# q projected two tiles ahead, in front of V, with a semaphore of its own for V's projections

## The chip, the cores and the metric

The kernel runs on one core of a Trainium2 chip. The metric is the device time of one execution in microseconds (us). A core has five engines that run beside each other and meet at semaphores: TensorE (PE; its weight loads are PEld), VectorE (DVE), ScalarE (ACT), GpSimd (POOL) and SyncE (SP, which here issues DMAs). Each takes its own instructions strictly in the order in which the program gives them.

## The reference

Four residual blocks run over x [1, 2048, 128]: an attention, a feed-forward with quantized operands, a causal attention, and six layers of windowed attention with a feed-forward each. The change touches only these six layers. Cut to what matters:

```python
def attn_layer(x, Wqkv, qs, ksc, Wo):              # x [1, 2048, 128], 16 heads of 64
    q, k, v = jnp.split(x @ Wqkv, 3, -1)           # each [2048, 1024]
    q = l2norm(q) * qs
    k = l2norm(k) * ksc
    q = q * cos * scale + rotate_half(q) * sin * scale
    k = k * cos * inv + rotate_half(k) * sin * inv
    out = local_attention(q, k, v)                 # 32 queries see 64 keys, softmax
    return out @ Wo

for i in range(DEPTH):                             # DEPTH = 6
    x = attn_layer(shift_tokens(x), Wqkv[i], q_scale[i], k_scale[i], Wo[i]) + x
    x = ffn_layer(shift_tokens(x), ln_g[i], ln_b[i], W1[i], b1[i], W2[i], b2[i]) + x
```

## The kernel before

The program is written by hand: each engine has a function that gives its instructions in order, and waits on semaphores with written-out counts. No scheduler moves anything. `layers` holds the six layers. Layers 0 to 4 run in a loop over `l` in which the wait counts are computed in registers; the sixth is written out after it. In each layer `attend(l)` goes over 16 tiles T of 128 tokens, and `forward(l)` does the feed-forward over four chunks.

What a tile goes through (i is 0 for q, 1 for k, 2 for V; b is the half of 512 columns):

- PE `project` (L1013) makes q, k or V of a tile, two blocks each. q and k of every tile use the same two PSUM banks 0 and 1; V goes into the score banks 3 and 4, so it waits until the tile before has been subtracted (`s.sub`).
- ACT `squares` (L1217, twice), DVE `sum_squares` (L1362, twice), ACT `inverse_norms` (L1223, L1225) and DVE `normalise` (L1367, a bound on 16 numbers a row, then L1375 twice) make the l2 norm and write `qn`. There is one `square` buffer and one `norm` buffer for q and k. When L1375 is through, banks 0 and 1 are free.
- DVE `cosines` (L1383) and POOL `rotate` (L956, L957) multiply `qn` with the rotary tables. POOL adds q's two parts (L963), DVE adds k's (`add_rotated`, L1391), both into `hat`. One `sine` buffer serves both.
- PE `turn` (L1024) transposes `hat` through one bank in four rounds r (0 and 1 for q, 2 and 3 for k), and ACT `store_qk` (L1238, L1239, L1241) empties it after each; so PE and ACT take turns.
- PE `scores` (L1035, L1042), DVE `maxima` (L1397) and `subtract` (L1403), ACT `exponentials` (L1253), DVE `sums` (L1410 and the reciprocal L1412), POOL `normalise_weights` (L980).
- A tile later: PE `turn_weights` (L1057), ACT `place_low` (L1259) and DVE `place_high` (L1419), PE `values` (L1075), ACT `store_o` (L1267). Two tiles later: PE `out_project` (L1086) and DVE `residual` (L1426). The second `turn_weights` of a tile shares its bank with `out_project` and so waits for `residual`.

In step T the engines go as follows. PE: project q of T+1 (b 0), turn 0, project q (b 1), turn 1, out_project of T-2, turn 2, turn 3, turn_weights of T-1, project k of T+1, scores of T, values of T-1, project V of T+1. ACT: squares q (b 0), store_qk 0, squares q (b 1), store_qk 1, inverse_norms q, store_qk 2 and 3, place_low, squares and inverse_norms k, store_o, exponentials, store V (`store_values`, L1229). DVE: sums of T-1, sum_squares q, add_rotated, normalise and cosines q, residual, place_high, sum_squares and normalise k, maxima, subtract, cosines k.

Before the layers a small block makes a layer norm; in it SP issues three loads, clears the 32 semaphores of the stages before (L863) and waits for the loads.

## Time and profile before

| | |
|---|---|
| median of 3 runs | 4037.26 us |
| lowest, highest | 4025.07, 4046.39 us |
| profiled execution, its own time | 4047.98 us |
| its span (first to last instruction) | 4046.1 us |
| mean granted TensorE clock | 0.935 of 2.4 GHz |
| PE, DVE, ACT, POOL busy, share of the span | 77%, 72%, 52%, 28% |

The trace is of one execution, and its own time lies 10.7 us above the median. The span is the trace's; the time holds what lies around it too. A busy share is an average over stages with different limits, so the steps of the layers are read one by one. A row of the time line gives start and length in us, engine, line, operation, what is written and read, how many were merged, and in brackets the idle time of the engine before it with what ended it.

### The profile page before, as it was taken

Reading aid. Unit: us, or ns where it says so; the run is one execution under the profiler, and the core shown is the slowest. Engines: PE = TensorE matmul, PEld = TensorE weight load, DVE = VectorE, ACT = ScalarE, POOL = GpSimd, SP = SyncE. Lnnn points to the kernel's source line nnn. Section 1 sums busy time; section 2 is a strip of 40 time slices with the busy share of each in tenths; the row PEclk is TensorE's granted clock in tenths of the full one; section 3 lists DMA queues with packets and bytes.
Section 4 is the critical chain, followed back from the end, with each engine's and each line's share of the span. In section 5 each row is a group of like instructions: output and inputs, shape, how many; then the busy total and the mean of one; then the engine's idle time right before and its main releaser. Section 6 shows DMA issues by size and latency. Waiting matters only on the chain. (4 is left out here: it accounts for less than half of the span.)

```text
span 4046.1 us, 67071 instructions
## 1 busy us (share of the span) xinstructions
PE 3125.7 (77%) x25619; PEld 1597.3 (39%) x25853; DVE 2893.7 (72%) x4198; ACT 2117.6 (52%) x3147; POOL 1116.3 (28%) x627
## 2 busy tenths in 40 slices
PE   3899999994433888966777777777877777777887
PEld 1122222221321333324554555355545535554554
DVE  4888888875742788846775777677677767776775
ACT  2366666664221455654664565465556646654664
POOL 2000000000020000015553555355345535553551
PEclk7799999997666999988999999999999999999999
DMA  3200000000023000001111101000110011110100
GB/s 93 37 1 1 1 1 1 1 1 6 0 72 46 2 1 1 1 33 41 30 30 34 33 27 45 26 27 28 39 33 28 27 34 34 32 44 22 32 27 22
DMA packets 56649, 100.33 MB, mean 25 GB/s; under 512 B 19782, under 2 KB 38148, under 8 KB 54916
## 3 DMA queue, kind: packets, MB, share of 16 engines
q1 hardware_dynamic: 56324, 95.92, 9.2%
q8 instruction: 214, 3.51, 0.4%
q14 instruction: 111, 0.91, 0.1%
HBM read 37.95 MB, written 7.34 MB: 11 GB/s over the span
## 5 line engine op out<-in xcount | busy, mean ns | idle before, releaser
L456 DVE TENSOR_REDUCE a_part<-ps 128x1 f32<-128x512 f32 (+3 forms) x1664 | 1010.9, 656 | 343.3 <-PE ps L330 310.4
L440 ACT ACTIVATE a_Pb<-ps 128x1024 f32<-128x1024 f32 (+3 forms) x832 | 778.3, 973 | 640.6 <-PE ps L406 634.2
L1013 PE MATMUL ps<-l_w_qkv,l_XS 128*128 128x512 f32 x1152 | 586.0, 632 | 206.8 <-DVE l_weights L1403 163.0
L330 PE MATMUL ps<-a_KS,a_QS 128*128 128x512 bf16 (+3 forms) x1592 | 567.5, 385 | 102.4 <-DMA a_QS<-pieces 44.3
L956 POOL TENSOR_TENSOR l_sine<-l_qn,l_tab 128x512 f32<-128x512 f32 x192 | 341.4, 1778 | 776.8 <-DVE l_qn L1375 776.7
L406 PE MATMUL ps<-a_QS,a_KS 128*128 128x512 bf16 (+3 forms) x1598 | 466.9, 368 | 19.6 <-DVE a_part L456 7.1
L1362 DVE TENSOR_REDUCE l_norm<-l_square 128x8 f32<-128x512 f32 x384 | 262.0, 686 | 298.1 <-ACT l_square L1217 286.7
L383 PE MATMUL ps<-a_Pb,V 128*32 128x512 f32 (+3 forms) x3328 | 422.8, 580 | 2.6 <-ACT a_Pb L440 1.3
L330 PEld LDWEIGHTS ps<-a_KS,a_QS 128*128 128x128 bf16 x1664 | 145.2, 98 | 649.7 <-DVE a_part L456 573.1
L1024 PE MATMUL ps<-ident,l_hat 128*128 128x128 f32 x1536 | 252.0, 288 | 150.9 <-ACT l_kT L1241 67.2
L1013 PEld LDWEIGHTS ps<-l_w_qkv,l_XS 128*128 128x128 f32 x1152 | 206.5, 199 | 383.3 <-DVE l_weights L1403 175.5
L1024 PEld LDWEIGHTS ps<-ident,l_hat 128*128 128x128 f32 x1536 | 174.8, 144 | 321.7 <-ACT l_qT L1239 129.8
L980 POOL TENSOR_TENSOR l_weights<-l_weights,l_rcp 128x1024 f32<-128x1024 f32 x96 | 188.6, 1964 | 313.0 <-DVE l_rcp L1412 313.0
L1217 ACT ACTIVATE l_square<-ps 128x512 f32<-128x512 f32 x384 | 228.7, 597 | 81.6 <-PE ps L1013 78.6
L1375 DVE TENSOR_TENSOR l_qn<-ps,l_norm 128x512 f32<-128x512 f32 x384 | 247.4, 686 | 24.3 <-DVE l_norm L1367 0.2
L1383 DVE TENSOR_TENSOR l_cosine<-l_qn,l_tab 128x1024 f32<-128x1024 f32 x192 | 252.5, 1315 | 7.4 <-POOL l_tab L971 3.4
L957 POOL TENSOR_TENSOR l_sine<-l_qn,l_tab 128x512 f32<-128x512 f32 x192 | 244.5, 1273 | 0.0
L622 POOL MEMSET f_w<- 128x1120 f32 x1 | 1.0, 1032 | 863.3 <-POOLq L270 863.3
L1042 PE MATMUL ps<-l_kT,l_qT 128*64 128x64 f32 x6144 | 222.0, 225 | 14.6 <-issue 1.0
L963 POOL TENSOR_TENSOR l_hat<-l_cosine,l_sine 128x1024 f32<-128x1024 f32 x96 | 227.0, 2365 | 20.5 <-POOL l_sine L957 19.3
L1042 PEld LDWEIGHTS ps<-l_kT,l_qT 128*64 128x64 f32 x6144 | 195.4, 138 | 83.2 <-issue 83.2
L406 PEld LDWEIGHTS ps<-a_QS,a_KS 128*128 128x128 bf16 x1664 | 156.8, 98 | 162.3 <-ACT a_Pb L440 34.0
(184 smaller groups left out, 4605.5 us busy)
## 6 DMA issues: line engine op xcount, KB each, us to landing
l_V_earlier<-l_V SPq DMA_DIRECT2D x96, 384.0 KB, 3.5
l_V_earlier<-l_V SPq DMA_DIRECT2D x96, 128.0 KB, 3.4
l_w_qkv<-in_L_ffn_Wqkv_dram SPq DMA_DIRECT2D x6, 1536.0 KB, 8.2
pieces<-a_piece SPq DMA_DIRECT2D x12, 512.0 KB, 2.6
a_KS<-pieces SPq DMA_DIRECT2D x48, 128.0 KB
a_QS<-pieces SPq DMA_DIRECT2D x48, 128.0 KB
l_w_o<-in_L_ffn_Wo_dram SPq DMA_DIRECT2D x6, 512.0 KB, 3.9
a_cos<-in_c_cos_dram SPq DMA_DIRECT2D x2, 1024.0 KB, 5.4
```

The lines of the kernel that those rows point to most:

```text
L330: mm = e.matmul(bank[:, 0:width], QS[:, c, head, qt * P:(qt + 1) * P], KS[:, head, b * CH:b * CH + width], start=not masked, stop=True, sk ...
L383: mm = e.matmul(O[32 * h:32 * h + 32, a:CH], t.V[:, kt, w:w + 32], Pb[:, n % 2, h, a:CH], start=(kt == 0), stop=(kt == tiles_of(c) - 1), s ...
L406: mm = e.matmul(ps[:, h, a:CH], KS[:, head, kt * P:(kt + 1) * P], QS[:, c, head, a:CH], start=not diagonal, stop=True, skip_group_check=di ...
L440: e.activation(Pb[:, n % 2, 2 * p:2 * p + 2, a:CH], ps[:, 2 * p:2 * p + 2, a:CH], ACT.Exp)\
L456: e.tensor_reduce(part[:, u % 2, h * TC + qt, b:b + 1], ps[:, 4 + n % 2, 0:width], AX.X, ALU.max)\
L956: e.tensor_tensor(sine[:, :, 0:ROT], swap[:, :, ROT:LD], table[:, :, 0:ROT], ALU.mult).then_inc(s.rotated, 1)
L1013: e.matmul(ps[:, (V_BANK[T] if i == 2 else 0) + b, :], XS[:, T * P:(T + 1) * P], w_qkv[:, at:at + CH], start=True, stop=True).then_inc(s.a ...
L1024: tr = e.transpose(ps[:, TURN_BANK, j * P:(j + 1) * P], hat[:, i, at:at + P], t.ident[:, :])
L1042: mm = e.matmul(ps[half:half + LD, bank, at:at + LD], qT[:, T % 2, j, w, :, :], kT[:, T % 2, j, WIN * w:WIN * (w + 2)], start=False, stop= ...
L1362: e.tensor_reduce(norm[:, 0, heads], square[:, heads, :], AX.X, ALU.add).then_inc(s.total, 1)
L1375: e.tensor_tensor(qn[:, i, heads, :], ps[:, b, :].rearrange("p (h d) -> p h d", h=HALF), norm[:, 3, heads].unsqueeze(2).to_broadcast([P, H ...
L1383: e.tensor_tensor(cosine[:, i, :, :], qn[:, i, :, :], tab[:, 2 * i, T, :].unsqueeze(1).to_broadcast([P, LH, LD]), ALU.mult).then_inc(s.cos ...
```

## The change

In step T the kernel now projects q of tile T+2 behind the values of T-1 and in front of V of T+1; before, it projected q of T+1 at the head of the step, its two blocks around the first turn. Everything that belongs to q's norm moves along:

- ACT: squares of q(T+2) in front of exponentials(T), its inverse_norms behind them.
- DVE: sum_squares of q(T+2) behind subtract(T). Behind them follow cosines of k(T+1), sums(T), add_rotated(T+1), and only then normalise and cosines of q(T+2).
- POOL: rotate of q(T+2) behind normalise_weights(T).
- Step 0 does the same work for q of tile 1 at its head, unsplit. Steps 14 and 15 have no q left to make.
- V's projections count on `v_ready` instead of `a_ready`, since the order of the counts changed. SP's load of the next layer's weights waits on `v_ready`.
- The 32 semaphore clears go into a block of their own ahead of the layer norm's block.

```diff
@@ SP @@
+        with nc.Block() as block:
+            @block.sync
+            def _(e):
+                for signal in t.spent:
+                    e.sem_clear(signal)
...
-                    for signal in t.spent:
-                        e.sem_clear(signal)
...
-                    e.wait_ge(s.a_ready, START + l * (6 * NT))
+                    e.wait_ge(s.v_ready, START + l * (2 * NT))
@@ POOL attend @@
+                    rotate(l, 1, 0)
                     for T in range(NT):
                         if T + 1 < NT:
-                            for i in range(2):
-                                rotate(l, T + 1, i)
+                            rotate(l, T + 1, 1)
                         normalise_weights(l, T)
+                        if T + 2 < NT:
+                            rotate(l, T + 2, 0)
@@ PE attend @@
-                        if ahead:
-                            project(l, T + 1, 0, 0)
+                        if T == 0:
+                            project(l, 1, 0, 0)
+                            project(l, 1, 0, 1)
                         turn(l, T, 0)
-                        if ahead:
-                            project(l, T + 1, 0, 1)
                         turn(l, T, 1)
...
                             values(l, T - 1, 1)
+                        if T + 2 < NT:
+                            project(l, T + 2, 0, 0)
+                            project(l, T + 2, 0, 1)
                         if ahead:
                             project(l, T + 1, 2, 0)
                             project(l, T + 1, 2, 1)
@@ ACT attend @@
-                        if ahead:
-                            squares(l, T + 1, 0, 0)
-                        store_qk(l, T, 0)
-                        if ahead:
-                            squares(l, T + 1, 0, 1)
-                        store_qk(l, T, 1)
-                        if ahead:
-                            inverse_norms(l, T + 1, 0)
-                        store_qk(l, T, 2)
-                        store_qk(l, T, 3)
+                        if T == 0:
+                            squares(l, 1, 0, 0)
+                            squares(l, 1, 0, 1)
+                            inverse_norms(l, 1, 0)
+                        for r in range(4):
+                            store_qk(l, T, r)
...
+                        if T + 2 < NT:
+                            squares(l, T + 2, 0, 0)
+                            squares(l, T + 2, 0, 1)
                         exponentials(l, T)
+                        if T + 2 < NT:
+                            inverse_norms(l, T + 2, 0)
@@ DVE attend @@
-                        if T:
-                            sums(l, T - 1)
-                        if ahead:
-                            sum_squares(l, T + 1, 0)
-                        if T:
-                            add_rotated(l, T)
-                        if ahead:
-                            normalise(l, T + 1, 0)
-                            cosines(l, T + 1, 0)
+                        if T == 0:
+                            sum_squares(l, 1, 0)
+                            normalise(l, 1, 0)
+                            cosines(l, 1, 0)
...
                         subtract(l, T)
+                        if T + 2 < NT:
+                            sum_squares(l, T + 2, 0)
                         if ahead:
                             cosines(l, T + 1, 1)
-                    sums(l, NT - 1)
+                        sums(l, T)
+                        if ahead:
+                            add_rotated(l, T + 1)
+                        if T + 2 < NT:
+                            normalise(l, T + 2, 0)
+                            cosines(l, T + 2, 0)
```

How it moves the instructions is shown at two places. The first is DVE in a middle tile of a looped layer, from subtract on. ISA and REGISTER_ALU rows are the sequencer's work on wait counts. Before:

```order
L1403 TENSOR_TENSOR l_weights<-ps,l_nmax 128x1024
L1383 TENSOR_TENSOR l_cosine<-l_qn,l_tab 128x1024
L1410 TENSOR_REDUCE l_total<-l_weights 128x16
L1412 RECIPROCAL l_rcp<-l_total 128x16
L1361 ISA
L1362 TENSOR_REDUCE l_norm<-l_square 128x8
L1361 REGISTER_ALU
L1362 TENSOR_REDUCE l_norm<-l_square 128x8
L1388 ISA
L1389 REGISTER_ALU
L1390 ISA
L1391 TENSOR_TENSOR l_hat<-l_cosine,l_sine 128x1024
```

The same engine and place after the change, where lines stand ten further down (L1413 is subtract, L1372 sum_squares, L1401 add_rotated):

```order
L1413 TENSOR_TENSOR l_weights<-ps,l_nmax 128x1024
L1371 ISA
L1372 TENSOR_REDUCE l_norm<-l_square 128x8
L1371 REGISTER_ALU
L1372 TENSOR_REDUCE l_norm<-l_square 128x8
L1393 TENSOR_TENSOR l_cosine<-l_qn,l_tab 128x1024
L1420 TENSOR_REDUCE l_total<-l_weights 128x16
L1422 RECIPROCAL l_rcp<-l_total 128x16
L1398 ISA
L1399 REGISTER_ALU
L1400 ISA
L1401 TENSOR_TENSOR l_hat<-l_cosine,l_sine 128x1024
```

The two reduces of q's squares moved from between the reciprocal and add_rotated to just behind subtract; add_rotated now stands right behind the reciprocal.

The second place is PE in a middle tile, from the last values of the tile before to out_project. Before:

```order
L1075 MATMUL ps<-l_wT,l_V 64x2x32 x2
L1013 MATMUL ps<-l_w_qkv,l_XS 128x512 x2
L1009 ISA
L1013 MATMUL ps<-l_w_qkv,l_XS 128x512
L1020 ISA
L1021 ISA
L1024 MATMUL ps<-ident,l_hat 128x128 x4
L1013 MATMUL ps<-l_w_qkv,l_XS 128x512
L1021 REGISTER_ALU
L1024 MATMUL ps<-ident,l_hat 128x128 x4
L1082 REGISTER_ALU
L1086 MATMUL ps<-l_oT,l_w_o 128x128 x8
```

After (L1082 is values, L1020 project, L1031 turn, L1093 out_project):

```order
L1082 MATMUL ps<-l_wT,l_V 64x2x32 x2
L1016 ISA
L1020 MATMUL ps<-l_w_qkv,l_XS 128x512 x4
L1027 ISA
L1028 ISA
L1031 MATMUL ps<-ident,l_hat 128x128 x4
L1028 REGISTER_ALU
L1031 MATMUL ps<-ident,l_hat 128x128 x4
L1089 REGISTER_ALU
L1093 MATMUL ps<-l_oT,l_w_o 128x128 x8
```

The four projections now stand in a row, q's two ahead of V's two, and nothing but the turns is left between V and out_project.

## Rows read from the trace of the kernel before

**Rows 1.** Windows: length, busy us (count) of PE, PEld, DVE, ACT, POOL; clock; DMA.

```profile
2309.67:2328.68 19.01, 15.12 (x181) 10.51 (x182) 14.83 (x21) 11.64 (x21) 10.21 (x7) 1.00 0.10 30
...
2231.00:2252.00 21.00, 16.49 (x165) 10.46 (x166) 14.18 (x20) 11.69 (x21) 9.86 (x7) 0.84 0.21 51
```

**Rows 2.** Time line of DVE, one step of layer 1, subtract to subtract.

```profile
2308.44 1.23 DVE L1403 TENSOR_TENSOR l_weights<-ps,l_nmax 128x1024 f32<-128x1024 f32 x1
2309.58 1.42 DVE L1383 TENSOR_TENSOR l_cosine<-l_qn,l_tab 128x1024 f32<-128x1024 f32 x1
...
2312.17 0.25 DVE L1412 RECIPROCAL l_rcp<-l_total 128x16 f32<-128x16 f32 x1
...
2315.00 0.69 DVE L1362 TENSOR_REDUCE l_norm<-l_square 128x8 f32<-128x512 f32 x1 [0.99 <-ACT l_square L1217]
2315.60 1.22 DVE L1391 TENSOR_TENSOR l_hat<-l_cosine,l_sine 128x1024 f32<-128x1024 f32 x1
2316.97 0.18 DVE L1367 TENSOR_SCALAR l_norm<-l_norm 128x16 f32<-128x16 f32 x1 [0.15 <-ACT l_norm L1225]
...
2319.76 0.28 DVE L1426 TENSOR_TENSOR X<-X,ps 128x128 f32<-128x128 f32 x1
...
2324.54 0.30 DVE L1367 TENSOR_SCALAR l_norm<-l_norm 128x16 f32<-128x16 f32 x1 [0.71 <-ACT l_norm L1225]
...
2327.45 1.23 DVE L1403 TENSOR_TENSOR l_weights<-ps,l_nmax 128x1024 f32<-128x1024 f32 x1
```

**Rows 3.** Time line of PE, the same step.

```profile
2309.72 2.84 PE L1013 MATMUL ps<-l_w_qkv,l_XS 128*128 128x512 f32 x6 [1.67 <-DVE l_weights L1403]
...
2320.10 0.65 PE L1057 MATMUL ps<-ident,l_weights 128*128 128x128 f32 x4 [0.73 <-DVE X L1426]
2320.59 1.88 PE L1013 MATMUL ps<-l_w_qkv,l_XS 128*128 128x512 f32 x4
...
2326.76 0.29 PE L1075 MATMUL ps<-l_wT,l_V 128*64 128x64 f32 x4
```

**Rows 4.** Time line of ACT, the same step.

```profile
2309.70 1.06 ACT L1253 ACTIVATE l_weights<-l_weights 128x1024 f32<-128x1024 f32 x1 [1.02 <-DVE l_weights L1403]
2311.74 1.01 ACT L1229 COPY l_V<-ps 128x1024 f32<-128x1024 f32 x1 [0.98 <-PE ps L1013]
...
2321.75 0.60 ACT L1217 ACTIVATE l_square<-ps 128x512 f32<-128x512 f32 x1 [0.38 <-PE ps L1013]
2322.51 0.60 ACT L1217 ACTIVATE l_square<-ps 128x512 f32<-128x512 f32 x1 [0.17 <-PE ps L1013]
```

**Rows 5.** Time line of POOL, the same step.

```profile
2312.50 1.90 POOL L980 TENSOR_TENSOR l_weights<-l_weights,l_rcp 128x1024 f32<-128x1024 f32 x1 [2.58 <-DVE l_rcp L1412]
...
2322.45 2.37 POOL L963 TENSOR_TENSOR l_hat<-l_cosine,l_sine 128x1024 f32<-128x1024 f32 x1 [0.24 <-POOL l_sine L957]
```

**Rows 6.** Time line of all engines behind the reciprocal of tile 14.

```profile
2133.91 0.25 DVE L1412 RECIPROCAL l_rcp<-l_total 128x16 f32<-128x16 f32 x1
2134.20 1.23 DVE L1391 TENSOR_TENSOR l_hat<-l_cosine,l_sine 128x1024 f32<-128x1024 f32 x1
2134.24 2.94 POOL L980 TENSOR_TENSOR l_weights<-l_weights,l_rcp 128x1024 f32<-128x1024 f32 x1 [2.58 <-DVE l_rcp L1412]
```

**Rows 7.** One line's instructions: count, ns min/median/max, first and last start.

```profile
L1367 DVE TENSOR_SCALAR l_norm<-l_norm x192: 174/176/1970, 1829.6 to 3964.1; 128x16 f32<-128x16 f32 x192
```

**Rows 8.** Time line, layer 2's tables on POOL beside a copy of DVE.

```profile
2522.60 7.18 POOL L971 TENSOR_TENSOR l_tab<-l_base,l_scales 128x1024 f32<-128x1024 f32 x3
...
2527.60 2.46 DVE L1434 COPY l_XS<-X 64x512 f32<-64x512 f32 x1
```

**Rows 9.** Time line of ACT, first tile of layer 1.

```profile
2214.67 0.60 ACT L1217 ACTIVATE l_square<-ps 128x512 f32<-128x512 f32 x1
2215.16 0.57 ACT L1238 COPY l_qT<-ps 64x512 f32<-64x512 f32 x1
```

**Rows 10.** One line's instructions: the semaphore clears of SP.

```profile
L863 SPq EVENT_SEMAPHORE_RANGE_CLEAR  x32: 25/25/34, 1796.4 to 1798.1; - x32
```

More of the change, by code:

```diff
@@ L807, in layers @@
     with ExitStack() as ctx:
-        s = semaphores(ctx, nc, "l_", "w_qkv w_tab w_o w_mlp xs tab a_ready square total root qn cosine v_done rotated "
+        s = semaphores(ctx, nc, "l_", "w_qkv w_tab w_o w_mlp xs tab a_ready v_ready square total root qn cosine v_done rotated "
                        "t_ready t_free s_ready nmax sub exp_done sums rcp normed p_ready low high earlier_even earlier_odd "
@@ L998, in _ @@
                 e.sem_inc(s.a_ready, START)
+                e.sem_inc(s.v_ready, START)
                 e.sem_inc(s.t_ready, START)
@@ L1013, in project @@
                     e.matmul(ps[:, (V_BANK[T] if i == 2 else 0) + b, :], XS[:, T * P:(T + 1) * P], w_qkv[:, at:at + CH],
-                             start=True, stop=True).then_inc(s.a_ready, 1)
+                             start=True, stop=True).then_inc(s.v_ready if i == 2 else s.a_ready, 1)
                 def turn(l, T, r):
@@ L1213, in squares @@
                     n = (l * NT + T) * 2 + i
-                    e.wait_ge(s.a_ready, START + (l * NT + T) * 6 + 2 * i + b + 1)
+                    e.wait_ge(s.a_ready, START + (l * NT + T) * 4 + 2 * i + b + 1)
                     if b == 0:
@@ L1227, in store_values @@
                 def store_values(l, T):
-                    e.wait_ge(s.a_ready, START + (l * NT + T) * 6 + 6)
+                    e.wait_ge(s.v_ready, START + (l * NT + T) * 2 + 2)
                     e.copy(V[:, T % 3, :], flat2(ps[:, V_BANK[T]:V_BANK[T] + 2, :])).then_inc(s.v_done, 1)
```

## The prediction

> **What bounds the kernel now.** I read the busy shares, then the windows, then the time line of one step, engine by engine. The windows show that no engine is full: in a step of 19.01 us PE is busy 15.12, DVE 14.83, ACT 11.64, POOL 10.21 [rows 1]. So a chain across engines sets the step, and the time line shows it. Let S be the end of subtract (L1403), 2309.67; times below are from S. The next S is 19.01 later [rows 2].
>
> - V's projection starts at S + 0.05, and q's two blocks queue behind it, with a turn between them. PE had idled 1.67 for subtract [rows 3].
> - q's second square comes late on ACT, behind a store_qk. DVE waits 0.99 for it, so add_rotated (L1391) starts at 5.93, though its reciprocal ended at 2.75 [rows 2].
> - Then the bound L1367 at 7.30, normalise, cosines, and residual (L1426) ends at 10.37 [rows 2]. PE has waited 0.73 for residual with the second turn_weights, which starts at 10.43; project k follows at 10.92 [rows 3].
> - From there k's squares, norm, maxima and subtract lead to the next S.
>
> So residual's end on DVE is the gate, and DVE reaches it late because of q's squares. From residual to the next S nothing is changed but the q projections, which lie beside it.
>
> **The change, step by step (middle tiles).**
>
> PE: q's two projections of T+2 go into the idle time before V. The last values row starts at -1.92 (2326.76 against 2328.68), its four matmuls give way in about 0.1, so q starts near -1.81. Four records at 0.43 end their issue near -0.1; V, due at +0.05, is not late, but by a margin of only 0.15. Banks 0 and 1 are free, since k is normalised before maxima.
>
> ACT: the squares start 1.16 and 1.92 after a pair's first matmul (2320.59 to 2321.75 and 2322.51) [rows 3, 4], so at -0.65 and 0.11; the second ends at 0.71. Exponentials (1.06) then end at 1.8 instead of 1.1 and q's two small activations near 2.4; the V copy starts there instead of at 2.07 [rows 4]. The next store_qk is not held up by squares any more, so the turns come out some 0.4 earlier. This branch had the 0.73 of slack before turn_weights, and now has more.
>
> DVE: the first reduce fits at once, the second waits for its square until 0.74 and ends at 1.43. Cosines of k start at 1.35. From L1383 to L1412 it was 2.59, of which 0.20 (1.42 against the 1.22 of the equally large L1391) was a wait for POOL, which is through by now. So the reciprocal starts at 3.74 and ends at 3.99, 1.24 later than before.
>
> Now the place on which the sum rests. Behind the reciprocal stand add_rotated on DVE and normalise_weights (L980) on POOL. Before, this pair met only at tile 14, where no q is left: L1391 started 0.29 after the reciprocal's start, L980 0.04 later, and L980 took 2.94 instead of 1.90 [rows 5, 6]. So the two don't run together: the later one stands still. In every middle tile add_rotated will run from 4.03 to 5.26, and L980 will end as in rows 6, 3.02 after the reciprocal's end, at 7.01. Next on DVE is q's bound L1367. It takes 0.18, but 1.97 at worst [rows 7], and 0.30 beside POOL's L963, ending 0.02 behind it [rows 2, 5]: it waits for POOL too. Who goes first when add_rotated ends, POOL's waiting L980 or DVE's next one? At 2527 POOL had three L971 in a row and DVE's copy L1434 took 2.46, until the one that had waited was through [rows 8]. So L980 first: the bound ends near 7.03, not 5.4. From the bound's end to residual's end it was 2.89 (2317.15 to 2320.04) [rows 2], so residual ends at 9.92 instead of 10.37. **The step gains 0.45**, where the idle time removed promised over 1.
>
> POOL: q's L963 ends before k's bound, which it already held up by 0.12. It follows cosines of q and comes 0.45 earlier too, so this branch agrees.
>
> The Trainium skill (SBUF — State Buffer, Who interferes with whom) says that a VectorE instruction with two SBUF inputs, or a tensor_scalar in a two-port mode, and a GpSimd instruction that reads SBUF exclude each other, and that issue order decides who blocks. The trace agrees (2.94 against 1.90). It speaks against this order of instructions: without the rule the bound would be through at 5.4 and the step would gain over 1 us.
>
> **Ends of the layers.** Steps 0 to 2 and 14 to 15 differ; 12 intervals of a layer are middle ones: 12 x 6 x 0.45 = 32 us.
> - Step 0: the first store_qk stood behind one square (2214.67, 2215.16) [rows 9]. Now it stands behind both, DVE's second reduce and two small activations: 0.60 + 0.69 + 0.65 and the hops, 2.1 us later, and all turns and k's projection with it. It costs 2.1 a layer.
> - The two intervals after it have no residual to wait for, or a nearly free one, so PE's own queue counts, which lost a split q: an estimate of 0.5 to 1 each, the more as these tiles run at a granted clock of 0.84 [rows 1], where the shorter queue behind subtract is worth more. I take 1.6 for both, so 0.5 lost a layer, 3 in all; bounds 0 and 12.
> - Steps 14 and 15 have the old order. `v_ready` changes no moment: V's last projection was the last count of `a_ready` as well.
> - The clears: 32 in 1.7 us, hidden so far beside the layer norm [rows 10]. Now DVE waits for them: 2 us with a second barrier, once.
>
> Sum: 32 - 3 - 2 = 27 us. Against the profiled execution's 4048 that gives 4021; it lay 10.7 above the median, so against the median of 4037 I say **4010**.
>
> **Rivals.**
> 1. *The bound slips in ahead of L980.* For it: DVE's next instruction starts up to 0.09 before the one in front ends (L1383 at 2309.58, L1403's end at 2309.67), so it might find the shared path still DVE's. Against it: L980 has then been waiting for 1.1 us. DVE would gain 1.6 more, and the PE and ACT branch would become the bound with some 0.7 more than my forecast: 1.1 a step, 79 - 5 = 74 us, 3963.
> 2. *L980 gets in ahead of add_rotated.* The lead is 0.04 us [rows 6]. Then add_rotated waits until 5.9 and ends at 7.13, the bound behind it at 7.2 instead of 7.03: 0.28 a step, 20 - 5 = 15, 4022.
> 3. *The wait comes back whole.* If q's squares come 0.45 later than I place them (an unseen wait of PE ahead of q, or values that end later), the reciprocal moves by as much and nothing is gained: the 5 us of the ends remain, 4042.
> 4. *Slower: the clock.* At a layer's start the granted clock is 0.84 and a step takes 21.0 [rows 1], 2 us more. Step 0 now leaves PE idle longer between its turns, and more tiles could run at 1.2 GHz instead of 2.4. It costs about 2 a step; from 14 more such steps, some 2 or 3 a layer, the gain is gone, and with 4 a layer (48 us) it is 21 us slower, 4058. Against it: middle steps show 1.00 and get denser.
>
> **How the numbers follow.** My forecast 0.58 (4000 to 4022, with 0.3 to 0.55 a step), rival 1 0.12, rival 2 0.11, rival 3 0.11, rival 4 0.08. A measurement of this kernel can tell some 0.5%, 20 us, from no change: 4017. Faster by more: rival 1, most of the forecast's range, a little of rival 2, 0.62. Within: 0.31. Slower: 0.07. The range for 8 in 10 takes in rival 3 and stops short of rivals 1 and 4: 3975 to 4042.
>
> **What would show it.** Middle steps of 18.5 to 18.6 between two subtracts (19.01 before). L980 at 2.9 in nearly all tiles instead of 1.90, starting 0.04 behind add_rotated. L1367 of q at about 1.8, ending with L980. PE idle before V near 0.1, not 1.67. First store_qk of a layer 2.1 later. Wrong if q's L1367 stays at 0.18 and the step falls to 18 (rival 1), if add_rotated takes 3 (rival 2), if the reciprocal ends 4.4 or more behind subtract (rival 3), or if the clock of a layer's first tiles falls below 0.84 for more of them (rival 4).

## The result

| | before | after |
|---|---|---|
| median, us | 4044.43 (8 runs, 4025.07 to 4059.36) | 4073.10 (8 runs, 4066.66 to 4096.35) |
| ratio to before, 95% interval | | 1.0079 [1.0052, 1.0107] |
| profiled execution, its span | 4046.1 | 4072.9 |
| mean granted clock | 0.935 | 0.917 |

The change makes the kernel 0.8% slower. The forecast was 4010, faster; the time lies above its range. A ratio leaves out a kernel's executions that lie more than 1.5% above its fastest, which is four of twelve in experiment 9 and four of six in experiment 11, the profiled ones among them, so I give the ratio of the medians there too.

Where the 26.8 us between the two spans lie, measured from subtract to subtract in both traces:

| stretch | before | after | difference |
|---|---|---|---|
| ahead of the last layer norm (code that is not changed, and after it the block of clears, 2.1) | 1793.2 | 1801.4 | +8.2 |
| from there to the first subtract of layer 0 | 71.6 | 76.3 | +4.7 |
| five gaps, last subtract of a layer to first of the next | 423.8 | 439.4 | +15.6 |
| first two intervals of the six layers | 242.7 | 224.8 | -17.9 |
| 72 middle intervals | 1364.0 | 1380.2 | +16.2 |
| last interval of each layer, and the end | 150.8 | 150.8 | 0 |

The first row is no measurable effect of the change: experiment 1, which has all of the change outside the tiles, costs nothing that can be measured, and the same code takes 1760.4 to 1808.3 in the profiles of the kernels below.

### The profile page after: what moved, and what is told of

Its sections match the earlier page's. It is cut to its first block and busy times, and to the rows that moved or that the text cites. A ratio compares the mean times of both kernels' runs of the same rounds, so it can differ in the third digit from the quotient of the medians.

```text
span 4072.9 us, 66713 instructions
## 1 busy us (share of the span) xinstructions
PE 3155.9 (77%) x25619; PEld 1638.4 (40%) x25853; DVE 3006.9 (74%) x4198; ACT 2093.2 (51%) x3147; POOL 1197.5 (29%) x627
## 5 line engine op out<-in xcount | busy, mean ns | idle before, releaser
L1020 PE MATMUL ps<-l_w_qkv,l_XS 128*128 128x512 f32 x1152 | 593.9, 652 | 61.0 <-DVE l_qn L1385 18.4
L406 PE MATMUL ps<-a_QS,a_KS 128*128 128x512 bf16 (+3 forms) x1598 | 467.9, 369 | 24.4 <-DMA a_QS<-a_mrow 10.8
L1031 PE MATMUL ps<-ident,l_hat 128*128 128x128 f32 x1536 | 261.1, 296 | 277.6 <-ACT l_qT L1248 209.8
L1372 DVE TENSOR_REDUCE l_norm<-l_square 128x8 f32<-128x512 f32 x384 | 261.1, 685 | 205.0 <-ACT l_square L1226 195.7
L984 POOL TENSOR_TENSOR l_weights<-l_weights,l_rcp 128x1024 f32<-128x1024 f32 x96 | 269.2, 2805 | 435.9 <-DVE l_rcp L1422 435.9
L1031 PEld LDWEIGHTS ps<-ident,l_hat 128*128 128x128 f32 x1536 | 187.2, 150 | 383.7 <-ACT l_qT L1248 196.1
L1020 PEld LDWEIGHTS ps<-l_w_qkv,l_XS 128*128 128x128 f32 x1152 | 214.9, 204 | 289.1 <-issue 170.5
L1385 DVE TENSOR_TENSOR l_qn<-ps,l_norm 128x512 f32<-128x512 f32 x384 | 247.4, 686 | 24.3 <-DVE l_norm L1377 0.2
L1393 DVE TENSOR_TENSOR l_cosine<-l_qn,l_tab 128x1024 f32<-128x1024 f32 x192 | 236.6, 1232 | 7.4 <-POOL l_tab L975 3.4
L1377 DVE TENSOR_SCALAR l_norm<-l_norm 128x16 f32<-128x16 f32 x192 | 177.6, 925 | 77.3 <-ACT l_norm L1234 77.3
L1049 PEld LDWEIGHTS ps<-l_kT,l_qT 128*64 128x64 f32 x6144 | 195.5, 138 | 88.7 <-issue 88.7
```

Source lines behind the costliest of these rows:

```text
L406: mm = e.matmul(ps[:, h, a:CH], KS[:, head, kt * P:(kt + 1) * P], QS[:, c, head, a:CH], start=not diagonal, stop=True, skip_group_check=di ...
L984: e.tensor_tensor(weights[:, T % 2, :, :], weights[:, T % 2, :, :], rcp[:, :].unsqueeze(2).to_broadcast([P, LH, LD]), ALU.mult).then_inc(s ...
L1020: e.matmul(ps[:, (V_BANK[T] if i == 2 else 0) + b, :], XS[:, T * P:(T + 1) * P], w_qkv[:, at:at + CH], start=True, stop=True).then_inc(s.v ...
L1031: tr = e.transpose(ps[:, TURN_BANK, j * P:(j + 1) * P], hat[:, i, at:at + P], t.ident[:, :])
L1049: mm = e.matmul(ps[half:half + LD, bank, at:at + LD], qT[:, T % 2, j, w, :, :], kT[:, T % 2, j, WIN * w:WIN * (w + 2)], start=False, stop= ...
L1372: e.tensor_reduce(norm[:, 0, heads], square[:, heads, :], AX.X, ALU.add).then_inc(s.total, 1)
```

## The profile after

A middle step of layer 1, from the subtract that ends at S = 2338.43. First DVE (start, length, engine, line, operation; the lines of before are in [rows 2]):

```profile
2337.21 1.22 DVE L1413 TENSOR_TENSOR l_weights<-ps,l_nmax 128x1024 f32<-128x1024 f32 x1
2338.62 1.45 DVE L1372 TENSOR_REDUCE l_norm<-l_square 128x8 f32<-128x512 f32 x2 [0.19 <-ACT l_square L1226]
...
2342.37 0.25 DVE L1422 RECIPROCAL l_rcp<-l_total 128x16 f32<-128x16 f32 x1
2342.67 1.23 DVE L1401 TENSOR_TENSOR l_hat<-l_cosine,l_sine 128x1024 f32<-128x1024 f32 x1
2343.82 1.87 DVE L1377 TENSOR_SCALAR l_norm<-l_norm 128x16 f32<-128x16 f32 x1
2345.84 1.29 DVE L1385 TENSOR_TENSOR l_qn<-ps,l_norm 128x512 f32<-128x512 f32 x2
...
2348.30 0.28 DVE L1436 TENSOR_TENSOR X<-X,ps 128x128 f32<-128x128 f32 x1
```

And POOL beside it ([rows 5] and [rows 6] of before):

```profile
2342.70 2.96 POOL L984 TENSOR_TENSOR l_weights<-l_weights,l_rcp 128x1024 f32<-128x1024 f32 x1 [4.00 <-DVE l_rcp L1422]
```

add_rotated (L1401) and normalise_weights (L984) start 0.03 apart and L984 takes 2.96 instead of 1.90. q's bound L1377, 16 numbers a row, takes 1.87 instead of 0.18 and ends at 2345.69, 0.03 behind L984. So the three collide as forecast. But the reciprocal ends at S + 4.19, not 3.99, and residual (L1436) at S + 10.15, not 9.92.

PE in the same step:

```profile
2336.74 3.73 PE L1020 MATMUL ps<-l_w_qkv,l_XS 128*128 128x512 f32 x8
2340.30 0.60 PE L1031 MATMUL ps<-ident,l_hat 128*128 128x128 f32 x4
2342.85 0.66 PE L1031 MATMUL ps<-ident,l_hat 128*128 128x128 f32 x4 [1.95 <-ACT l_qT L1248]
2343.34 2.87 PE L1093 MATMUL ps<-l_oT,l_w_o 128*128 128x128 f32 x16
```

The eight projection records now run in a row, and nothing is left between the first and the second turn (L1031): PE is idle there for 1.95 us. Before, half of q's projection stood in this place. And out_project (L1093) takes 2.87 here; at full clock it takes 1.95. In layer 3 it is k's projection that is hit:

```profile
3137.25 0.60 PE L1064 MATMUL ps<-ident,l_weights 128*128 128x128 f32 x4
3139.00 0.71 PE L1064 MATMUL ps<-ident,l_weights 128*128 128x128 f32 x4 [1.14 <-DVE X L1436]
3139.50 3.57 PE L1020 MATMUL ps<-l_w_qkv,l_XS 128*128 128x512 f32 x4
```

3.57 instead of the 1.88 of [rows 3]: that is the 1.2 GHz level. The windows of these two steps (length, busy PE, PEld, DVE, ACT, POOL, clock, DMA; compare [rows 1]):

```profile
2338.44:2357.21 18.77, 16.00 (x182) 11.68 (x182) 16.23 (x20) 11.16 (x22) 11.25 (x7) 0.91 0.10 29
3134.00:3154.48 20.48, 16.54 (x183) 11.09 (x184) 16.20 (x21) 11.38 (x22) 11.24 (x7) 0.92 0.10 28
```

Both have a stretch at half clock in them, and the mean clock is nearly the same. Their PE busy time holds the lengthened instructions: a step of after that is at full clock throughout (2282.02 to 2300.79) has PE busy for 14.86 of 18.77. In the first it lies on out_project, which has 1.1 us of slack ahead of the second turn_weights, and the step takes the 18.77 that it takes without. In the second it lies on k's projection, on the path, and the step takes 1.7 more. From tile 6 of layers 3 and 4 on, every middle step has its half-clock stretch at S + 10.8 and takes 20.47; in the last layer every second tile has one, and steps alternate between 18.47 and 19.17. Added up from the granted clock over the trace, middle steps have 116.0 us at half clock, in 34 stretches: 16 on k's projection, which cost 1.7 each, and 18 on out_project and the turns beside it, which cost 0.7 or less in the last layer and some 0.15 at most in the others. Before they had none.

Two lines of the page, groups by line (count, busy, mean ns, idle before with its releaser); before, project (L1013) had 206.8 idle ahead of it, 163.0 of it for subtract, and turn (L1024) 150.9:

```profile
L1020 PE MATMUL ps<-l_w_qkv,l_XS 128*128 128x512 f32 x1152 | 593.9, 652 | 61.0 <-DVE l_qn L1385 18.4
L1031 PE MATMUL ps<-ident,l_hat 128*128 128x128 f32 x1536 | 261.1, 296 | 277.6 <-ACT l_qT L1248 209.8
```

146 us of idle time ahead of the projections went away, and 127 us came back ahead of the turns.

## The experiments

All ran with before beside them on the same chip. "Middle" is the sum of the 72 middle intervals, "half clock" the time at 1.2 GHz in middle steps, both from the profiled execution.

| kernel | ratio to before | middle | gaps | half clock |
|---|---|---|---|---|
| before | 1 | 1364.0 | 423.8 | 0 |
| after | 1.0079 [1.0052, 1.0107] | 1380.2 | 439.4 | 116.0 |
| 1 before, side edits | 1.0007 [0.9975, 1.0040] | 1366.0 | 420.9 | 3.4 |
| 2 no bound of q | 0.9785 [0.9733, 0.9837] | 1275.3 | 439.7 | 47.8 |
| 3 two matmuls between the turns | 0.9986 [0.9950, 1.0023] | 1348.5 | 430.2 | 0 |
| 4 out_project between the turns | 1.0260 [1.0206, 1.0313] | 1455.1 | 439.1 | 259.4 |
| 5 first tile as before | 1.0016 [0.9985, 1.0046] | 1387.9 | 415.1 | 105.8 |
| 6 before, q unsplit | 1.0121 [1.0075, 1.0167] | 1416.2 | 435.8 | 0 |
| 7 bound early | 0.9796 [0.9744, 0.9848] | 1281.2 | 443.0 | 51.2 |
| 8 bound early, 3 and 5 | 0.9622 [0.9579, 0.9664] | 1261.7 | 406.9 | 0 |
| 9 one matmul between the turns | 0.9962 [0.9920, 1.0004] | 1375.7 | 432.6 | 54.6 |
| 10 one matmul behind out_project | 1.0090 [1.0057, 1.0123] | 1380.4 | 429.1 | 88.7 |
| 11 3 and 5 | 0.9891 [0.9819, 0.9963] | 1365.3 | 406.4 | 34.1 |
| 12 8, V copied later | 0.9605 [0.9570, 0.9640] | 1236.1 | 406.3 | 0 |

### 1. The edits outside the tiles, alone

The kernel before, with the block of clears ahead of the layer norm, `v_ready`, and SP's wait on it.

> The kernel before, with only the two side edits of the change: the 32 semaphore clears in a block of their own ahead of the layer norm, and V's projections counted on v_ready. No instruction of the layers stands elsewhere. Theory (the order of the work is what costs): 2 us slower at most, 1.7 us of clears and a barrier, so a ratio of 1.000 to 1.001; middle steps stay at 19.0 with the clock at 1.00. Rival (the side edits cost part of the 29 us): 1.003 or more, seen ahead of the first subtract.

Measured 1.0007 [0.9975, 1.0040], middle steps of 19.0, with one stretch at half clock in layer 0, where a step takes 20.69. These edits cost nothing that can be measured; whatever the change does, its order in the tiles does it.

### 2. Without q's bound

```diff
-    e.tensor_scalar(norm[:, 3, :], norm[:, 2, :], 1.0 / NORM_MIN, None, ALU.min)
+    if i:    # k only; q's normalise reads norm[:, 2, :]
+        e.tensor_scalar(norm[:, 3, :], norm[:, 2, :], 1.0 / NORM_MIN, None, ALU.min)
```

> The kernel after, in which q's norm is used without the bound of 1e12 (one instruction of 16 numbers a row on VectorE left out for q, kept for k). It takes away the instruction that stood 1.9 us still behind add_rotated beside GpSimd's normalise_weights. Theory A (this wait on the path between add_rotated and residual costs the rest of the gain): normalise of q starts 1.6 us earlier, the next two-input instruction, cosines, then waits for GpSimd until 7.2 after subtract, and residual ends near 8.6 instead of 10.3; the step falls from 18.78 by 0.5 to 1.0, to what the turns of TensorE and ScalarE allow. Rival (TensorE's clock is all that matters): the step of a full-clock tile stays at 18.78, since the turns bind as well.

Measured 0.9785 [0.9733, 0.9837], and a step of 17.42 at full clock instead of 18.77. DVE behind the reciprocal, where S is 2340.76:

```profile
2344.83 0.25 DVE L1423 RECIPROCAL l_rcp<-l_total 128x16 f32<-128x16 f32 x1
2345.13 1.22 DVE L1402 TENSOR_TENSOR l_hat<-l_cosine,l_sine 128x1024 f32<-128x1024 f32 x1
2346.28 1.28 DVE L1386 TENSOR_TENSOR l_qn<-ps,l_norm 128x512 f32<-128x512 f32 x2
2347.59 1.61 DVE L1394 TENSOR_TENSOR l_cosine<-l_qn,l_tab 128x1024 f32<-128x1024 f32 x1
2349.12 0.28 DVE L1437 TENSOR_TENSOR X<-X,ps 128x128 f32<-128x128 f32 x1
```

normalise (L1386), which reads PSUM and one SBUF operand, runs right behind add_rotated and beside normalise_weights; only cosines (L1394), with two SBUF operands, stands still until POOL is through, and it loses just 0.38 (1.61 against 1.23). residual ends at S + 8.64 instead of 10.15. So the wait behind POOL was held by one instruction of 16 numbers a row, and it cost 1.35 a step (0.9 in the last layer): over 90 us in all, three times what my forecast had wanted to gain.

### 3. Two matmuls between the turns

```diff
                         turn(l, T, 0)
+                        if T and T + 1 < NT:
+                            for b in range(2):
+                                e.matmul(ps[:, Y_BANK, :], t.ident[:, :], <base, 512 columns>, start=True, stop=True)
                         turn(l, T, 1)
```

Nothing reads the product; out_project writes the bank anew behind it.

> The kernel after, with two 128x512 matmuls of constants (results never used) put between the first and the second turn of tiles 1 to 14, where TensorE idled 1.95 us and where its second q projection had stood before the change. It adds about 1.7 us of TensorE work a step and takes no wait away. Theory B (that idle time is what lets the granted clock fall in the middle steps): the 116 us at half clock in middle steps go to nearly none, the steps of 20.47 in layers 3 and 4 go to 18.8, and the kernel gets 20 to 30 us faster in spite of the added work. Rival (the clock falls for another reason, such as the idle time around turns 2 and 3): the half-clock time stays above 60 us and the kernel gets slower, since the fill takes 3.4 us where the clock is halved.

Measured 0.9986 [0.9950, 1.0023]. PE in the place, layer 1:

```profile
2329.77 0.60 PE L1031 MATMUL ps<-ident,l_hat 128*128 128x128 f32 x4
2330.21 1.88 PE L1120 MATMUL ps<-l_base,ident 128*128 128x512 f32 x4
2332.32 0.66 PE L1031 MATMUL ps<-ident,l_hat 128*128 128x128 f32 x4 [0.23 <-ACT l_qT L1251]
2332.81 1.95 PE L1093 MATMUL ps<-l_oT,l_w_o 128*128 128x128 f32 x16
```

The twelve middle intervals of layer 3 as one window, after and then this kernel:

```profile
3012.58:3251.51 238.93, 192.69 (x2169) 132.47 (x2180) 194.37 (x242) 135.88 (x252) 133.93 (x73) 0.93 0.10 28
```

```profile
2998.13:3223.51 225.38, 199.46 (x2229) 133.27 (x2228) 195.55 (x242) 136.27 (x252) 134.05 (x73) 1.00 0.10 29
```

13.6 us less in this layer, at a clock of 1.00 instead of 0.93, with the same work on DVE, ACT and POOL and more on PE. Useless matmuls make the kernel some 37 us faster (0.0093 of 4024). The higher clock stands in every execution and not only in the profiled one: its mean is 0.930 to 0.937 in this kernel's twelve, and 0.913 to 0.919 in the eight of after. Middle steps average 18.78, and 18.47 in the last layer: that is what the new order gives at full clock, 15.5 us less than before over all middle intervals.

### 4. out_project between the turns

```diff
                         turn(l, T, 0)
-                        turn(l, T, 1)
                         if T >= 2:
                             out_project(l, T - 2)
+                        turn(l, T, 1)
```

> The kernel after, with out_project (16 matmuls, 1.95 us, its input ready long before) moved from behind turn 1 to between turn 0 and turn 1. The idle time of 1.95 is filled with work that has to be done anyway. Theory B: the half-clock stretches of the middle steps are gone, all middle steps at 18.8 or a little less, since turn 2 no longer waits behind out_project; 25 to 40 us faster than the kernel after, so near 0.998 of the kernel before. Rival: idle time only moves to between turn 1 and turn 2, the clock falls as often as before, within 5 us of the kernel after.

A clear miss: 1.0260 [1.0206, 1.0313]. I had wanted to cover the idle time with work that is there anyway. But out_project had covered another: between the second and the third turn PE is now idle for 1.26, and for 1.44 ahead of the second turn_weights. The clock falls there instead, behind the turns and on k's projection in nearly every tile, 259.4 us in all, and layer 3's middle window takes 245.90 at 0.90. So covering one stretch with work taken from the next does not help. The idle time between the first two turns is 0.19 here and the clock falls most often, so it is not that one gap by itself: the rest of the way to k's projection counts too.

### 5. The first tile of a layer as before

In step 0 alone, PE: project q (b 0), turn 0, project q (b 1), turn 1. ACT: squares, store_qk 0, squares, store_qk 1, inverse_norms.

> The kernel after, but step 0 of every layer has the old order: PE projects q of tile 1 around the first turn, ACT squares one half, empties the first turn, squares the other half, empties the second turn, and makes the inverse norms then. The middle steps are the kernel after. My theory: the stretch between the last subtract of a layer and the first of the next is 3.1 us longer after (439.4 against 423.8 us for five of them, and 52.8 against 48.1 ahead of layer 0) because the first store_qk stands behind both squares and the norm. Then it comes back to 424 to 426 and 48 to 49: 17 us less, and the intervals 0 to 1 of the layers (112.1 us for six) lose little of their gain over before (125.9). Rival: the stretch is longer since the projection of q of tile 2 stands in front of V of tile 1; then it stays at 437 to 441 and the time does not change.

Measured 1.0016 [0.9985, 1.0046], 0.0063 under after: some 25 us. The gaps fall by 24.3, more than the 15 expected, and below those of before. In the profile the middle intervals take 7.7 more than in after, since layers 3 and 4 now have steps of 20.47 from tile 2 on. What I had not seen is the clock again. In before, k's projection in step 0 of layer 1 takes 3.62 and V's waits 3.72:

```profile
2221.24 3.62 PE L1013 MATMUL ps<-l_w_qkv,l_XS 128*128 128x512 f32 x4
...
2231.43 0.83 PE L1013 MATMUL ps<-l_w_qkv,l_XS 128*128 128x512 f32 x1 [3.72 <-DVE l_weights L1403]
```

In this kernel k's projection takes 1.88, and q of tile 2 stands in the idle time ahead of V, of which 0.44 and 1.00 are left:

```profile
2217.31 1.88 PE L1020 MATMUL ps<-l_w_qkv,l_XS 128*128 128x512 f32 x4
...
2222.33 1.98 PE L1020 MATMUL ps<-l_w_qkv,l_XS 128*128 128x512 f32 x4 [0.44 <-DVE l_qn L1390]
2225.32 1.12 PE L1020 MATMUL ps<-l_w_qkv,l_XS 128*128 128x512 f32 x2 [1.00 <-DVE l_weights L1418]
```

The gaps have 52.8 us at half clock before, 68.3 after and 30.7 in this kernel. So the unsplit start cost more than its own delay: PE is idle for 3.24 between its first two turns in the kernel after,

```profile
2230.84 0.66 PE L1031 MATMUL ps<-ident,l_hat 128*128 128x128 f32 x4 [3.24 <-ACT l_qT L1248]
```

and what comes behind runs at half clock.

### 6. The kernel before, with q unsplit

PE projects both halves of q of T+1 ahead of turn 0; all else is before.

> The kernel before, with one edit: PE projects both halves of q of tile T+1 ahead of the first turn, so nothing stands between the first and the second turn. ACT and DVE keep the order of before. Theory (the idle time between the turns lets TensorE's clock fall): the granted clock in some middle steps falls below 1.00 here too, where it was 1.00 in all of them before; half-clock time in middle steps 100 to 400 us instead of 3, and steps of 20.4 instead of 19.0 where k's projection is hit: 4050 to 4130 us, ratio 1.005 to 1.025. Rival (the clock falls since the new order packs the step and moves q away from the middle of it, the idle time alone does not do it): middle steps stay at 19.0 and the clock at 1.00, ratio 0.998 to 1.003.

Neither theory holds. Middle steps are slower, 19.72, but at a clock of 1.00 throughout:

```profile
2358.49 3.70 PE L1013 MATMUL ps<-l_w_qkv,l_XS 128*128 128x512 f32 x8 [1.68 <-DVE l_weights L1402]
2362.03 0.60 PE L1024 MATMUL ps<-ident,l_hat 128*128 128x128 f32 x4
2363.89 0.66 PE L1024 MATMUL ps<-ident,l_hat 128*128 128x128 f32 x4 [1.26 <-ACT l_qT L1238]
```

The edit does not rebuild the idle time that I wanted: the first turn waits behind four more records, the second comes at its heels, and PE is idle for 1.26 between them, not 1.95. The 0.72 a step is that later first turn, with everything behind it on ACT. So this run neither supports nor refutes the cause of the fallen clock; it shows that in the old order the split was worth 0.72 a step. One thing more it shows: PE is busy for 15.12 of 19.72 in such a step, a smaller share than in the full-clock steps of before (15.12 of 19.01) or after (14.86 of 18.77), and yet the clock stays up. The busy share of a whole step does not tell whether it falls.

### 7. The bound, early

```diff
                         if ahead:
                             cosines(l, T + 1, 1)
+                        if T + 2 < NT:
+                            bound(l, T + 2, 0)
                         sums(l, T)
                         if ahead:
                             add_rotated(l, T + 1)
```

`normalise` of q no longer makes the bound (in tiles 0 and 1 it still does). Nothing is left out.

> The kernel after, but DVE's bound of q's norm (128x16 elements) stands ahead of the sums of the exponentials, so behind cosines of k and in front of normalise_weights on POOL, instead of behind add_rotated and beside normalise_weights. Nothing is left out. Theory (what holds q's normalise is only that this one small instruction waits for POOL): it takes 0.18 to 0.3 at its new place, the reciprocal and add_rotated come 0.2 later, normalise starts right behind add_rotated at 5.8 behind subtract instead of 7.4, residual ends near 8.8 instead of 10.15, and the step is 17.5 to 17.7 at full clock (18.77 after; 17.42 without the bound): ratio to before 0.978 to 0.986 with some steps at a fallen clock. Rival (the place behind cosines of k is not free, since rotate of POOL still runs there or the inverse norms come too late at 2.4): the bound costs 1 us there and the step gains only 0.3 to 0.5.

Measured 0.9796 [0.9744, 0.9848]. DVE, where S is 2317.82:

```profile
2320.63 0.17 DVE L1377 TENSOR_SCALAR l_norm<-l_norm 128x16 f32<-128x16 f32 x1
2320.71 1.21 DVE L1425 TENSOR_REDUCE l_total<-l_weights 128x16 f32<-128x1024 f32 x1
2321.95 0.25 DVE L1427 RECIPROCAL l_rcp<-l_total 128x16 f32<-128x16 f32 x1
2322.26 1.22 DVE L1406 TENSOR_TENSOR l_hat<-l_cosine,l_sine 128x1024 f32<-128x1024 f32 x1
2323.40 1.28 DVE L1390 TENSOR_TENSOR l_qn<-ps,l_norm 128x512 f32<-128x512 f32 x2
```

0.17 instead of 1.87, and the step is 17.42: as good as leaving the bound out, a little better than the 17.5 to 17.7 expected. PE no longer waits ahead of the second turn_weights (its eight matmuls run in one piece, 1.04), so residual no longer holds k's projection. One line moved up by three instructions turns a change of +0.8% into one of -2.0%.

### 8. Bound, filler and first tile together

> The early bound, the old order in step 0 of a layer, and two matmuls of 128x512 between the first and the second turn in tiles 1 to 14 whose result nothing reads. Theory: the three effects add, since they lie at different places: 1.15 us a middle step (83 us against the full-clock steps of the kernel after), no half-clock time in middle steps (34 us against after), and 17 us at the layers' starts: 3910 to 3940 us, ratio to before 0.970 to 0.979. Rival (the denser step lets the clock fall at another place, as it did when out_project was put between the turns: 259 us at half clock): middle steps alternate between 17.6 and 18.8 and the ratio is 0.980 to 0.988.

Measured 0.9622 [0.9579, 0.9664], a median of 3897.85, under the range expected. Middle steps 17.42 (17.55 in the last layer, and in each of the others one of 18.73 at full clock, the cause of which stays open), half clock 0, gaps 406.9. The effects add, and the layers' starts give more than I had put down: the gaps alone 32.5 against after, of which experiment 5 had shown 24.3.

### 9 and 10. One matmul, at two places

The same matmul of 128x512 (0.94 us), once between turn 0 and turn 1, once between the first and the second turn_weights, in tiles 1 to 14.

> The kernel after with one matmul of 128x512 (0.94 us of PE) instead of two between the first and the second turn in tiles 1 to 14; nothing reads its result. With none the middle steps had 116.0 us at half clock, with two they had 0. Theory (too little PE work between V's projections and k's projection lets the clock fall): the effect goes by amount, 0 to 50 us at half clock, and the time lies between those two, ratio to before 0.998 to 1.004. Rival (only a full cover of the idle time between the turns helps): still 80 us or more and ratio 1.004 to 1.010.

> The kernel after with the same single matmul, but between the first and the second turn_weights, where PE is idle for 1.1 us behind out_project, and right ahead of k's projection, on which the fallen clock lay. Theory of the place (the idle time between the turns itself is what the clock falls for): the middle steps keep 80 to 150 us at half clock, ratio 1.004 to 1.012. Theory of the stretch (all PE work between V's and k's projection counts, wherever it stands): as few half-clock microseconds as with one matmul between the turns, ratio 0.998 to 1.004. Both: the step at full clock stays at 18.77 to 18.85, since PE was idle there for 1.14 us.

Between the turns 0.9962 [0.9920, 1.0004] (by medians 1.0023), behind out_project 1.0090 [1.0057, 1.0123] (by medians the same). After it stands at 1.0079, with two matmuls at 0.9986. So the place counts, and the amount. The mean clock says the same of every execution: 0.925 to 0.939 in the twelve with the matmul between the turns, 0.915 to 0.920 in the eight with it later. By the profiles one matmul between the turns takes off about half of the half-clock time (54.6 of 116.0), the same one later nothing of the time and 27 us of the half-clock time. What the later one does change is where the clock falls: never on k's projection, always on out_project, and since the idle time that had absorbed this is now filled, such a step takes up to 20.05. In the first case the profiled execution had the step of 20.47 in parts of layers 0 and 4, in after in layers 3 and 4. All its 16 stretches in middle steps lie on k's projection; gone are only those on out_project, which cost little, and the middle intervals are no more than 4.5 us shorter than in after. This execution took 4048.04, where the twelve range from 3984.48 to 4065.07, so that one matmul saves time rests on the ratio and the mean clocks, not on this trace.

### 11. Filler and first tile, without the early bound

> The kernel after with both repairs that touch what the forecast had missed: step 0 of a layer in the old order, and two matmuls between the turns in tiles 1 to 14. DVE, POOL and the middle steps' order are as after. My theory: what is left is what my forecast meant, a middle step of 18.77 (gain 0.23 instead of 0.45) and layer starts that give back nothing: middle intervals 1348 to 1352 us (1364.0 before), gaps between the layers 405 to 415 (423.8 before), ratio to before 0.990 to 0.995. Rival (the forecast was wrong in something else too, such as the cleared semaphores or the second interval of a layer): 0.996 to 1.000.

Measured 0.9891 [0.9819, 0.9963]; but its six executions spread from 3954.65 to 4040.81, and by medians it is 0.9993. The profile, of an execution of 4026.60, has gaps of 406.4 as expected and five layers at averages of 18.47 to 18.78, but layer 3 from tile 2 on nearly all at 20.47, 34.1 us at half clock, which makes the middle intervals 16.8 longer than in experiment 3. So two matmuls between the turns do not exclude the pattern: the profiles of experiments 3, 8 and 12 are free of it, this one has it in one layer. It does not explain the whole spread of 86 us. The code ahead of the last layer norm took 1808.3 in this profile, 48 more than in the shortest, and it has its own time at half clock (389.1 here, 342.9 in the shortest), so the mean granted clock (0.943 at 3954.65, 0.935 at 4004.89, 0.929 at 4040.81) does not tell the two apart. The full-clock part is as forecast by the sum of 3 and 5; neither the ratio nor that of the medians settles how much of the time it keeps.

### 12. V copied later, cosines of q behind residual

ACT empties V behind the second store_qk of the next step; DVE makes cosines of q behind residual. Otherwise kernel 8.

> The fastest kernel so far (early bound, old order in step 0, two matmuls between the turns) with two more moves: ACT copies V of tile T+1 out of PSUM behind the second store_qk of the next step, instead of ahead of the first one, and DVE makes cosines of q behind residual instead of ahead of it. Theory (with the early bound residual is no longer what PE waits for; the alternation of turns and store_qk is, which starts at 3.3 behind subtract because the V copy of 1.0 stands ahead of it): store_qk starts at 2.6, k's projection at 8.8 instead of 9.47, and the step is 16.7 to 16.9 instead of 17.42: 3840 to 3860 us, ratio to before 0.950 to 0.957. Rival (the turns are bound by add_rotated and normalise_weights, which end at 5.7 and 7.4): the step gains 0.2 or less, ratio 0.959 to 0.963.

Measured 0.9605 [0.9570, 0.9640], a median of 3863.88, the lowest of all; but its interval overlaps that of kernel 8. In the profiles the middle intervals fall by 25.6, to steps that average 17.20, where I had expected 16.7 to 16.9. Two things hold the rest. The two matmuls now stand in the way of turn 1, which starts at S + 4.12 though ACT is through at 3.77. And k's bound stands behind POOL, as q's had:

```profile
2311.64 0.57 DVE L1385 TENSOR_SCALAR l_norm<-l_norm 128x16 f32<-128x16 f32 x1 [0.72 <-ACT l_norm L1238]
```

```profile
2309.81 2.37 POOL L967 TENSOR_TENSOR l_hat<-l_cosine,l_sine 128x1024 f32<-128x1024 f32 x1 [0.24 <-POOL l_sine L961]
```

It ends at 2312.21, 0.03 behind POOL, the same pair as in [rows 5], now on the path.

## Why the prediction was wrong

**That residual's end is the gate, and q's squares hold it: right.** The step at full clock moved by what residual's end moved, 0.22 each (10.37 to 10.15, 19.00 to 18.78), and experiments 2 and 7 moved both again.

**The order on the shared path: right.** L984 at 2.96 (forecast 2.94), L1377 at 1.87 and ending with it (forecast about 1.8), both behind add_rotated. The median of L984 over the six layers is 2957 ns. The rule of the Trainium skill (SBUF — State Buffer, Who interferes with whom) that issue order decides who blocks fits this too: POOL had been waiting since 2342.70, the bound came behind it and ended 0.03 after it. Without that wait the step is 17.42, as experiments 2 and 7 show. Rival 1 is what experiment 7 makes of the kernel: I had priced it at 1.1 a step against before; it is 1.58 (19.00 to 17.42), 1.36 of it beyond what the kernel got.

**The gain of 0.45 a step: mis-sized, 0.22.** The terms were q's start (-1.81, measured -1.69) and the way from a first matmul to its square (1.16, measured 1.25). Each is small, but they stand in a chain that has no slack, and the reciprocal ends 0.20 later than I said. Half of the gain went with it: 15.5 us of the middle steps instead of 32. This is the half of rival 3.

**The layer starts: right in sum.** I had 3 us lost. That it comes out is luck in part, since both terms were off by some 1.3 a layer, in opposite directions. Measured: 4.7 and 15.6 lost ahead of the first subtract of a layer (3.4 a layer; I had 2.1), 17.9 gained in the two intervals behind it (3.0 a layer; I had 1.6), 2.4 in all. The loss was larger and I had no term for the clock in it; experiment 5 shows that the unsplit first tile costs some 25 us against one that keeps the old order there.

**The clears and `v_ready`: right.** Nothing measurable.

**The clock: wrong, and this decides.** The step that failed is the sentence against rival 4, "middle steps show 1.00 and get denser". It put the clock at nothing in the middle steps, and they do not get denser: at full clock PE is busy for 14.86 of 18.77 after and for 15.12 of 19.01 before, 79% and 80% (the 16.00 in the window of 18.77 above holds the instructions that ran at half clock). And the idle time that went was 1.67 long and stood ahead of V's projection, while what came for it is 1.95 in one piece between the first two turns, where the split half of q had stood; before, PE was idle for 0.54 ahead of the second turn (2314.40 in that trace). I had looked at this place only in step 0, where I wrote that it leaves PE idle longer; in the middle tiles my list of what moves on PE named only the place to which q's projections go and not the one they leave. The runs show the price: with two matmuls there, middle intervals fall by 31.7 us and the ratio from 1.0079 to 0.9986; with one, the ratio is 0.9962 (1.0023 by medians); with the same one behind out_project, 1.0090. Rival 4 had the mechanism and nearly the time (4058), but it expected the fallen steps at the layers' starts and 2 us each; 16 of them came in the middle of layers 3 and 4, at 1.7 each.

The sum in terms of the two profiles: I expected -27, measured +26.8. Of the 54 between them, 16.5 are the smaller gain of a step, 31.7 the clock in middle steps, 8.2 the code ahead of the layers with the clears in it, and -2.6 the layer starts with the 2 us that I had put down for the clears.

**Open.** What PE must do between V's and k's projection to keep its clock. That more plain matmuls between the first two turns keep it up is shown; that the length of this gap decides is not, since experiment 4 closes it and the clock falls more often, and kernel 7 keeps it (1.98) without the later idle time ahead of the second turn_weights and has 15 stretches instead of 34. The turns are transposes and what I put between them were not, so whether a transpose there would serve as well is open. Why layers 3 and 4 fall into steps of 20.47 and layers 1 and 2, with the same instructions, do not; kernel 11 has it in layer 3, kernel 9 in parts of 0 and 4. What the traces show is that a layer that has entered this pattern mostly stays in it to its end. And experiment 6 did not test the idle time in the old order, so all of this is shown for the new order only.

## What to carry to other kernels

When an instruction moves, cost the place that it leaves as closely as the one that it goes to: a matmul in the middle of a stretch with little PE work can be worth more than its own length, since what follows may run at half clock. Of the engines that share a path, look at what is queued right behind the pair that collides; if it is small and could stand ahead of the pair, moving it is nearly free (1.36 us a step here). And a gain that is a difference of two long chains needs each link from its own row: two links that were off by 0.1 took half of it. Compare PE's busy share between steps at the same granted clock only; an instruction at half clock makes a step look denser.

## What the runs showed of the hardware that I had not expected

- DVE's TENSOR_SCALAR of 128x16, 0.17 to 0.18 alone, takes 1.87 beside a POOL instruction that had been waiting for DVE; a TENSOR_TENSOR with one operand in PSUM (L1386 in experiment 2: 1.28 for two, 1.29 in the kernel after) does not wait beside the same POOL instruction.
- The granted clock of TensorE falls in steps whose full-clock neighbours have PE busy for 14.86 of 18.77, and does not fall in steps with 15.12 of 19.72 (experiment 6). Useless matmuls of 1.88 us a step repay themselves: 225.38 us instead of 238.93 for twelve steps.
- A loop can lock to the fallen clock: 20.47 a step for eight tiles on end with the half-clock stretch at the same instruction, and 18.77 for the same instructions elsewhere in the same execution.
